# Splitting seven key blocks instead of six in the first half of each head

## The reference

```python
x = x + attention(layernorm(x), ctx, ctx, gamma)   # 8 heads per sequence
x = x + ffn(layernorm(x))                          # relu router, softmax over 8 experts of rank 64
# attention, for each sequence and head: q, k and v are 128 rows of layernorm(x), ctx, ctx
qk = einsum('bhdq,bhdl->bhql', qh, kh) / sqrt(dq)  # the row is the depth, the 1,024 columns are positions
ret = einsum('bhql,bhdl->bhdq', softmax(qk), vh)
```

## Time and profile before

| | |
|---|---|
| three runs | 1506.14, 1514.12, 1512.76 us |
| median | 1512.76 us |
| the profiled execution | 1504.3 us, span from first to last instruction 1502.5 us |
| granted TensorE clock, mean | 0.998 of full |
| busy share of the span | TensorE 98%, VectorE 70%, ScalarE 55%, GpSimd 50% |
| attention | up to about 765 us of the span |
| weight loads of TensorE | 76% of the span |

### The profile page before, as it was taken

One profiled execution on the slowest core, in us unless ns is written; L12 is line 12 of the kernel. 1 busy time (PEld: TensorE's weight loads), 2 busy tenths in 40 slices (PEclk: granted clock), 3 DMA queues, 4 the chain that ended last, 5 costly groups with the idle time before them and its releaser, 6 DMA issues.

```text
span 1502.5 us, 20433 instructions
## 1 busy us (share of the span) xinstructions
PE 1479.0 (98%) x6212; PEld 1148.6 (76%) x6212; DVE 1053.4 (70%) x1295; ACT 820.2 (55%) x1264; POOL 755.7 (50%) x480
## 2 busy tenths in 40 slices
PE   7999999999999999999999999999999999999999
PEld 6777777777777777777667878878788887878877
DVE  8999899999899998999658546363554535545212
ACT  6988889989898988898753121111212112112110
POOL 4898898998998888988734201102020020200200
PEclk9999999999999999999999999999999999999999
DMA  6899989989999999998994663635546454463304
GB/s 202 279 268 286 311 276 284 310 290 300 293 291 299 278 291 297 284 292 265 279 358 147 198 215 108 240 120 192 183 136 229 137 195 154 153 211 125 112 1 140
DMA packets 144392, 339.17 MB, mean 226 GB/s; under 512 B 29456, under 2 KB 48912, under 8 KB 144336
## 3 DMA queue, kind: packets, MB, share of 16 engines
q1 hardware_dynamic: 126768, 290.83, 61.4%
q10 hardware_dynamic: 17568, 47.72, 9.0%
HBM read 136.88 MB, written 52.69 MB: 126 GB/s over the span
## 4 chain that ended last, share of the span: by engine, by line
PE 60%; DVE 12%; SPq 11%; issue 6%; DMA 6%; ACT 3%; POOL 1%; ACTq 1%; DVEq 0%; POOLq 0%
PE scores L1148 22%; PE scores L1179 12%; PE attended L1197 11%; SPq L235 9%; PE scores L605 7%; PE attended L634 5%; DVE pb L685 5%; DMA pt<-pb 4%; DVE neg_max L676 4%; PE attended L637 2%; DMA attended_rows<-att_out 2%; PE scores L1163 1%; ACT probs L465 1%; PE scores L1166 1%; SPq L241 1%
## 5 line engine op out<-in xcount | busy, mean ns | idle before, releaser
L362 POOL TENSOR_TENSOR pt_lo<-pt,pt_hi 128x512 fp32r<-128x512 f32 x254 | 466.5, 1850 | 88.8 <-ACT pt_hi L444 87.4
L685 DVE STREAM_TRANSPOSE pb<-probs 128x1024 f32<-128x1024 f32 x256 | 315.6, 1233 | 33.1 <-DMA pt<-pb 29.0
L465 ACT ACTIVATE probs<-scores,neg_max 128x1024 f32<-128x1024 f32 x256 | 285.4, 1115 | 65.8 <-DVE neg_max L676 61.7
L676 DVE TENSOR_REDUCE neg_max<-scores 128x1 f32<-128x1024 f32 x256 | 308.1, 1204 | 10.8 <-PE scores L605 10.1
L444 ACT ACTIVATE pt_hi<-pt 128x512 fp32r<-128x512 f32 (+1 forms) x256 | 214.9, 840 | 10.6 <-DMA pt<-pb 10.5
L605 PE MATMUL scores<-k_hi,q_hi 128*128 128x512 f32 x512 | 210.7, 493 | 5.6 <-ACT probs L465 2.2
L1094 ACT ACTIVATE hidden<-scores,b_col 128x512 f32<-128x512 f32 x64 | 44.0, 688 | 314.7 <-PE scores L1148 314.7
L1043 POOL TENSOR_TENSOR rstd<-var_eps,minus_half 128x1 f32<-128x1 f32 x28 | 15.1, 548 | 396.1 <-DVE var_eps L1260 396.1
L1148 PE MATMUL scores<-nt_hi,w_hi 128*128 128x512 f32 x512 | 200.3, 391 | 0.9 <-DVE w_lo L1228 0.9
L1148 PE MATMUL scores<-nt_lo,w_hi 128*128 128x512 f32 x512 | 199.9, 390 | 0.0
L1148 PE MATMUL scores<-nt_hi,w_lo 128*128 128x512 f32 x512 | 199.6, 390 | 0.0
(11 more groups left out here) (107 smaller groups left out, 2603.4 us busy)
## 6 DMA issues: line engine op xcount, KB each, us to landing
pt<-pb SPq DMA_DIRECT2D x512, 256.0 KB, 5.3
attended_rows<-att_out SPq DMA_DIRECT2D x64, 256.0 KB, 5.7
result<-x SPq DMA_DIRECT2D x64, 256.0 KB, 4.2
out<-result SPq DMA_DIRECT2D x64, 256.0 KB, 3.0
k_raw<-in_ctx ACTq DMA_DIRECT2D x30, 512.0 KB, 5.7
x_raw<-in_x ACTq DMA_DIRECT2D x30, 512.0 KB, 6.3
first_n<-attended_rows SPq DMA_DIRECT2D x28, 512.0 KB, 4.1
gain_wide<-gains SPq DMA_DIRECT2D x28, 512.0 KB, 5.4
```

What stands on the lines that cost most here:

```text
L362: nc.gpsimd.tensor_tensor(pt_lo[2 * parity + half][:, :, keys, :], pt[2 * parity + half][:, :, keys, :], as_f32(hi[half][q][:]), ALU.subtr ...
L465: nc.scalar.activation(probs[j % 2][:], scored[:], ACT.Exp, bias=neg_max[:, j:j + 1], accum_out=row_sum[b][:, j:j + 1]).then_inc(s_exp, 1)
L676: nc.vector.tensor_reduce(neg_max[:, j:j + 1], scored[:], AX_X, ALU.max, negate=True).then_inc(s_max, 1)
L685: nc.vector.transpose(pb[half][:, :, j % HALF, :], probs[j % 2][:]).then_inc(s_blocks, 1)
```

## The change

In the first half of each head seven key blocks are split and one is native; in the second half it stays six and two. The second quarter of the first half now has two key blocks (1 and 2) and no native one, the third has 3 and 4, the fourth 5 and 6; block 7 stays native in the first quarter. `v_hi`, `v_lo` and `v_raw` have seven blocks for this; `v_nat` keeps blocks 6 and 7, as the second half still needs both. To make room, `x_half` and `gain_row` share the place of `own_in_order`, `pt_hi1_3` (the last quarter's `pt_hi` of the second half) moves to a place ahead of `v_hi`, and `att_out0` takes a place in the region over which the weights are loaded later. For that last move SyncE waits for the last store of `att_out0` before it loads V.

```diff
-    SPLIT = 6
-    NAT = JB - SPLIT
+    SPLIT = (7, 6)
+    MOST, NAT = max(SPLIT), JB - min(SPLIT)
-    QUARTER_KEYS = ((0, 1), (1, 2), (2, 4), (4, 6))
+    QUARTER_KEYS = (((0, 1), (1, 3), (3, 5), (5, 7)), ((0, 1), (1, 2), (2, 4), (4, 6)))
...
-    hi.append([(top if q < 3 else place).tensor(f"pt_hi1_{q}", [P, QB, hi_k - lo_k, P], F32R)
-               for q, (lo_k, hi_k) in enumerate(QUARTER_KEYS)])
+    hi.append([top.tensor(f"pt_hi1_{q}", [P, QB, hi_k - lo_k, P], F32R)
+               for q, (lo_k, hi_k) in enumerate(QUARTER_KEYS[1][:3])])
+    att_out = [place.tensor("att_out0", [P, BANK])]
...
-    v_raw = place.tensor("v_raw", [P, SPLIT, P])
+    v_raw = place.tensor("v_raw", [P, MOST, P])
...
+    hi[1].append(place.tensor("pt_hi1_3", [P, QB, QUARTER_KEYS[1][3][1] - QUARTER_KEYS[1][3][0], P], F32R))
+    v_hi = [place.tensor(f"v_hi{b}", [P, MOST, P], F32R) for b in range(2)]
+    v_lo = [place.tensor(f"v_lo{b}", [P, MOST, P], F32R) for b in range(2)]
...
-    x_half = place.tensor("x_half", [P, BANK])
-    gain_row = place.tensor("gain_row", [P, BANK])
-    att_out = [place.tensor(f"att_out{b}", [P, BANK]) for b in range(2)]
+    att_out.append(place.tensor("att_out1", [P, BANK]))
...
     own = place.tensor("own", [P, L])
+    under = SbufMap(nc, place.at)
+    x_half, gain_row = under.tensor("x_half", [P, BANK]), under.tensor("gain_row", [P, BANK])
     own_in_order = place.tensor("own_in_order", [P, L])
...
         sp.wait_ge(s_pv, n)
+
+        sp.wait_ge(s_att[0], heads * 16)
         for tile, dram in shared["v_loads"]:
...
-            first_key, end_key = QUARTER_KEYS[q]
+            first_key, end_key = QUARTER_KEYS[half][q]
             for key in range(first_key, end_key):
                 for i in range(3):
...
-                             stop=(key == SPLIT - 1 and i == 2))
-            if q < NAT:
-                ins = mm(attended[half][:], v_nat[b][:, q, :], pt[at][:, :, SPLIT + q, :], start=False, stop=False)
+                             stop=(key == SPLIT[half] - 1 and i == 2))
+            if SPLIT[half] + q < JB:
+                key = SPLIT[half] + q
+                ins = mm(attended[half][:], v_nat[b][:, key - (JB - NAT), :], pt[at][:, :, key, :], start=False, stop=False)
```

More of the change, by code:

```diff
@@ L78, in attention @@
     pb = [place.tensor(f"pb{b}", [P, QB * JB, HALF, SB]) for b in range(2)]
-    hi = [[place.tensor(f"pt_hi{b}_{q}", [P, QB, hi_k - lo_k, P], F32R) for q, (lo_k, hi_k) in
-           enumerate(QUARTER_KEYS)] for b in range(1)]
+    hi = [[place.tensor(f"pt_hi0_{q}", [P, QB, hi_k - lo_k, P], F32R) for q, (lo_k, hi_k) in
+           enumerate(QUARTER_KEYS[0])]]
     top = SbufMap(nc, shared["top_at"])
-    hi.append([(top if q < 3 else place).tensor(f"pt_hi1_{q}", [P, QB, hi_k - lo_k, P], F32R)
-               for q, (lo_k, hi_k) in enumerate(QUARTER_KEYS)])
+    hi.append([top.tensor(f"pt_hi1_{q}", [P, QB, hi_k - lo_k, P], F32R)
+               for q, (lo_k, hi_k) in enumerate(QUARTER_KEYS[1][:3])])
+    att_out = [place.tensor("att_out0", [P, BANK])]
     assert place.at == shared["loaded_end"]
@@ L109, in attention @@
     place = SbufMap(nc, shared["nt_at"] + 8 * L * 4)
-    v_hi = [place.tensor(f"v_hi{b}", [P, SPLIT, P], F32R) for b in range(2)]
-    v_lo = [place.tensor(f"v_lo{b}", [P, SPLIT, P], F32R) for b in range(2)]
+    hi[1].append(place.tensor("pt_hi1_3", [P, QB, QUARTER_KEYS[1][3][1] - QUARTER_KEYS[1][3][0], P], F32R))
+    v_hi = [place.tensor(f"v_hi{b}", [P, MOST, P], F32R) for b in range(2)]
+    v_lo = [place.tensor(f"v_lo{b}", [P, MOST, P], F32R) for b in range(2)]
     v_nat = [place.tensor(f"v_nat{b}", [P, NAT, P]) for b in range(2)]
-    x_half = place.tensor("x_half", [P, BANK])
     probs = [place.tensor(f"probs{b}", [P, L]) for b in range(2)]
-    gain_row = place.tensor("gain_row", [P, BANK])
-    att_out = [place.tensor(f"att_out{b}", [P, BANK]) for b in range(2)]
+    att_out.append(place.tensor("att_out1", [P, BANK]))
     own = place.tensor("own", [P, L])
+    under = SbufMap(nc, place.at)
+    x_half, gain_row = under.tensor("x_half", [P, BANK]), under.tensor("gain_row", [P, BANK])
     own_in_order = place.tensor("own_in_order", [P, L])
@@ L220, in load_v @@
         def load_v(h):
-            sp.dma_start(v_raw[:, 0:SPLIT, :], ctx_t[rows_of(h), 0:SPLIT * P].rearrange("p (b d) -> p b d", d=P)
+            sp.dma_start(v_raw[:], ctx_t[rows_of(h), 0:MOST * P].rearrange("p (b d) -> p b d", d=P)
                          ).then_inc(s_v_in, 16)
         def load_v_native(h, parity):
-            sp.dma_start(v_nat[parity][:], ctx_t[rows_of(h), SPLIT * P:].rearrange("p (b d) -> p b d", d=P)
+            sp.dma_start(v_nat[parity][:], ctx_t[rows_of(h), (JB - NAT) * P:].rearrange("p (b d) -> p b d", d=P)
                          ).then_inc(s_vn_in, 16)
@@ L352, in low_values @@
             pool.wait_ge(s_vhi, h + 1)
-            nc.gpsimd.tensor_tensor(v_lo[b][:], v_raw[:, 0:SPLIT, :], as_f32(v_hi[b][:]), ALU.subtract).then_inc(s_vlo, 1)
+            nc.gpsimd.tensor_tensor(v_lo[b][:], v_raw[:], as_f32(v_hi[b][:]), ALU.subtract).then_inc(s_vlo, 1)
         def low_probs(quarter):
@@ L359, in low_probs @@
             count, half, q, _, parity = quarter
-            keys = slice(*QUARTER_KEYS[q])
+            keys = slice(*QUARTER_KEYS[half][q])
             pool.wait_ge(s_pthi, count + 1)
@@ L443, in high_probs @@
                 act.wait_ge(s_pv, count - (JB - 1))
-            nc.scalar.activation(hi[half][q][:], pt[2 * parity + half][:, :, slice(*QUARTER_KEYS[q]), :],
+            nc.scalar.activation(hi[half][q][:], pt[2 * parity + half][:, :, slice(*QUARTER_KEYS[half][q]), :],
                                  ACT.Copy).then_inc(s_pthi, 1)
@@ L453, in load_v @@
         def load_v(h):
-            act.dma_start(v_raw[:, 0:SPLIT, :], ctx_t[rows_of(h), 0:SPLIT * P].rearrange("p (b d) -> p b d", d=P)
+            act.dma_start(v_raw[:], ctx_t[rows_of(h), 0:MOST * P].rearrange("p (b d) -> p b d", d=P)
                          ).then_inc(s_v_in, 16)
         def load_v_native(h, parity):
-            act.dma_start(v_nat[parity][:], ctx_t[rows_of(h), SPLIT * P:].rearrange("p (b d) -> p b d", d=P)
+            act.dma_start(v_nat[parity][:], ctx_t[rows_of(h), (JB - NAT) * P:].rearrange("p (b d) -> p b d", d=P)
                          ).then_inc(s_vn_in, 16)
@@ L492, in high_values @@
                 act.wait_ge(s_pv, n - JB)
-            nc.scalar.activation(v_hi[b][:], v_raw[:, 0:SPLIT, :], ACT.Copy).then_inc(s_vhi, 1)
+            nc.scalar.activation(v_hi[b][:], v_raw[:], ACT.Copy).then_inc(s_vhi, 1)
         def gains(h, half):
@@ L722, in low_probs_end @@
         def low_probs_end(q):
-            keys = slice(*QUARTER_KEYS[q])
+            keys = slice(*QUARTER_KEYS[1][q])
             dve.wait_ge(s_pthi, heads * JB - HALF + q + 1)
```

## The result

The changed kernel takes 1517.03 us (median of 15 runs, 1512.11 to 1520.67) against 1509.93 us for the kernel before (15 runs, 1504.51 to 1514.12). The ratio is 1.0057, 95% interval 1.0045 to 1.0068: 7.1 us slower. Its profiled execution took 1516.52 us, at a granted clock of 0.999.

The account below looks back on a forecast made before the run. TensorE and the gathering ring were taken to bound it within 0.4 us, GpSimd nearly full; +7 to +14 over four loops less 1.2 gave +6 to +13, taken +9 on 1512.76: 1521 us, range 1506 to 1532.

Parts of the forecast that it names:

- the likeliest case: GpSimd's longer pieces and a later `q_lo` lengthen the loops: +9 us, 1521 to 1522, spanning 1517 to 1528; chance 0.55.
- The signs: Right if `q_lo` is 0.3 us or more longer, GpSimd over 95% busy in loops, loops 140 us or more.
- TensorE: First half of each head, a native key becomes split: -0.17 us a head, at most -5.3 over 31 heads.
- GpSimd and `q_lo`: Loops: GpSimd's pieces grow 1.38 us a head and push `q_lo` behind them: +1.7 to +3.5 us a loop.
- The sum of a loop: GpSimd's 131.3 us, six `q_lo` at 1.08 and waits of 2.4 to 4.2: 140.2 to 142.0 us.
- ScalarE: the step that failed: Grown quarter +0.42 and `v_hi` +0.10 us a head, costed at nothing; without cover 0.52 a head, 16 us.
- The end of attention: V's loads wait for the last head's first-half store, starting near 769 instead of 765.15: cost 0, at most 2 us.
- Transfers, addresses: 64 KB more a head: taken 0, up to 5.9 us, rival chance 0.10; shared addresses add no wait, cost 0.
- The sum: Whole kernel: four loops +7 to +14, seven heads without own rows give back 1.2: +6 to +13, taken +9 us.

Follow-up runs that it names:

- short piece: Changed kernel, but GpSimd subtracts only one of the two blocks in the first half's second quarter, and TensorE uses that result for both: 1.0025 against the kernel before.
- values: Changed kernel's addresses and store wait, six split blocks in both halves, but seven blocks of V loaded, rounded and subtracted, six used: 1.0026 against the kernel before.
- own short: GpSimd's own multiplications and additions cut from 128x512 to 32 columns, in both kernels: 1514.24 us changed, 1507.39 us before.
- `k_lo` short: GpSimd's low part of the keys cut to half its columns, in both kernels: 1.0055 changed, 1.0009 before, each against the uncut kernel before.
- `v_lo` short: Changed kernel with GpSimd's low part of the values cut from 896 to 384 columns: 1.0085 against the kernel before.
- second half: Changed kernel with seven split blocks in each head's later half instead, two in its first quarter, places moved, no store wait: 1.0143 against the kernel before.
- Places: Changed kernel's addresses and its wait for the store, with six split blocks in both halves: 1.0027 against the kernel before.
- seven where idle: Changed kernel, `v_nat` in the loaded region, no store wait, seventh block split only outside the loops and in steps 0 and 5: 1.0011 against the kernel before.

## Why the prediction was right, and where its sum was not

The time, 1517.0, is 4 us under the forecast of 1521 and at the lower end of the likeliest case (1517 to 1528; its own sum, 6 to 13 us on 1512.76, gives 1519 to 1526, and the prediction doesn't say where the rest comes from). Of the 4 us, 2.8 are the base: the kernel before has a median of 1509.93 in fifteen runs, 1512.76 in the first three. As a difference, +9 was forecast and +7.1 measured. The signs: loops are 140 us or more; GpSimd's wait for ScalarE fell from 45.4 to 15.2 us, and it is busy 96% in two of the four loops, 92 and 94% in the others, where over 95 was asked; `q_lo` is 0.25 us longer, where 0.3 or more was asked.

*TensorE.* Costed at -0.17 a head and worth little: the shortest heads are 0.22 shorter, and "short piece" is no faster than "values". Right in effect.

*GpSimd and `q_lo`.* +1.7 to +3.5 a loop from this cause alone. The loops of the profiles grew by 2.8, but GpSimd by itself shows in steps 2 to 4, with 1.8; relief to it brought 1.0 to 1.7 of that back there in four kernels (own short, `k_lo` short, `v_lo` short, short piece). More of it goes to the wait for `pt_lo` (5.6 to 21 us) than to `q_lo` (3.9 to 11), on which the prediction laid the weight; the second half shows that `q_lo` is the dearer place. The sum of a loop was 131.3 us of pieces and 8.9 to 10.7 of `q_lo` and waits; the loop from 269 us has 134.41 of pieces and 5.70 without. The time that `q_lo` takes from GpSimd shows as a longer next piece (128x512, 1410 ns on average instead of 1299), not as a gap: the total came out, its two terms didn't.

*ScalarE: the step that failed.* "I cost both at nothing", because ScalarE waits 14 us of a loop. That is a mean over six heads, and in step 5, from the second exponential to `q_hi`, there is nothing to wait with. The prediction named the price without that cover, 0.52 a head; step 5 is longer by 1.4, or by 1.07 in the mean of the nine kernels with the seventh block there against the five without (23.87 and 22.80): some 4 us over four loops, against 7 for GpSimd's 1.8 a loop, both from profiles. Not all of it is ScalarE's: 0.80 comes without the longer piece on GpSimd ("short piece" against "values"), and in the changed kernel GpSimd's row is as full in that head. How the two divide it, and why steps 0 and 1 give time back whenever GpSimd is relieved, stays open.

*The end of attention.* Cost 0, at most 2, and V's landing put 0.6 us behind its first use. The loads went out 4.0 us later against the first hidden product, as worked out, but ScalarE started 2.8 us later: 1.9 us by the profiles.

*Transfers, addresses.* "Places" and "values" are alike, so 0 was right for the 64 KB. "Places" is 4 us over before, of which 1.9 are the wait; no other cost of an address was found, and what is left isn't resolved.

*The sum.* In the two profiles, 2.4 us at the end, 4 x 2.83 in the loops and -1.6 in the outer heads make the 12.1 by which the spans differ. The medians differ by 7.1. The profile of before, at 1504.3, is 5.6 under its median of 15 runs, that of after 0.5 under its own, so the differences between these two are too large by some 5 us, which I can't share out among the parts.

So the forecast came out by errors that cancel: the one mechanism was given all of the loss, and a part of it lies elsewhere, in ScalarE's row and at the end of attention. No kernel here that computes everything beats the one before; "seven where idle", at 1.0011, would have had to leave step 5 out too, perhaps step 0 as well, which wasn't tried.

## What to carry to other kernels

An engine's idle time in a loop is no cover unless it stands in the head that pays: cut the windows by the kinds of step, and price a longer piece in the fullest one for each engine. When waits move from one producer to another and the time stays, several engines are full at once, and relief to one returns only where that one ended last. A tile lent into a region that a later stage loads ties that load to the tile's last user; lend the one whose last user is waited for anyway.

## What the runs showed of the hardware

VectorE's `q_lo` (two inputs in SBUF, 1.23 us alone) took 2.15 us on average when GpSimd's 2.4 us piece fell in its block, ending 1.09 us after it in the timeline above; GpSimd's next piece then took 1.62 instead of 1.29. The records show this as a pattern. Of 30 `q_lo` of 128x1024, 11 began while a piece of GpSimd ran in the kernel before, 24 in the changed one and all 30 in "second half"; in all but one in each of the last two they ended 1.08 to 1.12 us after that piece, however early they had begun. The six that found GpSimd free in the changed kernel took 1.19 to 1.23 us. VectorE's transposes `pb`, one input, stayed at 1231 and 1229 ns in the changed kernel and in "second half". The Trainium skill, "SBUF — State Buffer", section "Who interferes with whom", says that two-input VectorE instructions contend with GpSimd's reads of SBUF and that one-input ones outside the two-port modes don't; these numbers agree.
